# A decoder layer on one core: the first block's mean and variance in one-column instructions, and new sequences for all engines

## The reference

```python
x = _layernorm(x + attn(x))              # linear attention, width 128, with memory M, z
x = _layernorm(x + xattn(ctx, ctx, x))   # long convolution over the features, 32 heads of 8
x = _layernorm(x + ffn(x))               # 4-bit weights, 512 -> 2 x 1408 -> 512, RMS-normed

def _layernorm(x, axis=-1, eps=1e-05):
    m = jnp.mean(x, axis=axis, keepdims=True)
    v = jnp.var(x, axis=axis, keepdims=True)
    return (x - m) / jnp.sqrt(v + eps)
```

## Time and profile before

| | us |
|---|---|
| three runs: median (lowest to highest) | 527.06 (526.91 to 527.37) |
| the profiled execution | 527.41 |
| its span, first to last instruction | 525.7 |
| TensorE busy | 502.1 |
| VectorE, ScalarE, GpSimd busy | 378.5, 399.1, 384.1 |
| mean granted TensorE clock, share of full | 0.995 |

### The profile page before, as it was taken

How to read it: one execution, slowest core, us unless ns; L and a number is a source line. 1 busy time by engine, 2 the same in 40 slices (tenths; PEclk the granted TensorE clock), 3 DMA queues, 4 the chain that set the end, 5 groups by cost and what they waited for, 6 DMA issues and landing times.

```text
span 525.7 us, 11981 instructions
## 1 busy us (share of the span) xinstructions
PE 502.1 (96%) x3612; PEld 370.2 (70%) x3612; DVE 378.5 (72%) x1161; ACT 399.1 (76%) x962; POOL 384.1 (73%) x449
## 2 busy tenths in 40 slices
...
GB/s 222 182 18 82 131 99 111 109 100 46 1 58 135 144 117 66 39 64 97 66 26 85 67 80 20 83 57 80 22 130 8 40 38 43 2 2 40 1 22 40
DMA packets 91876, 36.45 MB, mean 69 GB/s; under 512 B 73851, under 2 KB 83195, under 8 KB 91835
## 3 DMA queue, kind: packets, MB, share of 16 engines
...
## 4 chain that ended last, share of the span: by engine, by line
PE 75%; ACT 8%; POOL 5%; DVE 4%; issue 3%; DMA 2%; SPq 2%; POOLq 0%; ACTq 0%; DVEq 0%
PE p_n L1271 6%; PE p_n L1270 6%; PE p_n L1269 6%; PE p_cv L129 6%; PE p_cv L131 6%; PE p_cv L130 6%; PE p_x L1256 5%; PE p_qk L1256 4%; PE p_x L1258 4%; PE p_qk L1258 4%; PE p_qk L870 4%; PE p_s L1256 4%; PE p_s L1258 3%; PE p_ct L101 2%; PE p_n L926 2%
## 5 line engine op out<-in xcount | busy, mean ns | idle before, releaser
L1109 ACT ACTIVATE p_qk<-p_qk,rescale 128x256 f32<-128x256 f32 x192 | 80.3, 471 | 22.3 <-PE p_qk L1258 20.8
L129 PE MATMUL p_cv<-kv_hi,toe 128*128 128x288 f16 x320 | 91.5, 286 | 2.3 <-issue 1.3
L131 PE MATMUL p_cv<-kv_hi,toe 128*128 128x288 f16 x320 | 91.5, 286 | 0.0
L130 PE MATMUL p_cv<-kv_lo,toe 128*128 128x288 f16 x320 | 91.5, 286 | 0.0
L1077 POOL TENSOR_TENSOR h_lo<-w,h_hi 128x256 f16<-128x256 f32 x88 | 63.6, 738 | 36.6 <-ACT h_hi L1126 36.5
L1109 ACT ACTIVATE p_x<-p_x,rescale 128x256 f32<-128x256 f32 x192 | 80.9, 480 | 0.6 <-PE p_x L1258 0.2
L283 POOL TENSOR_TENSOR shared<-shared 128x1024 f32<-128x1024 f32 x32 | 76.6, 2393 | 4.4 <-DVE shared L243 4.4
L1269 PE MATMUL p_n<-wd_hi,h_hi 128*128 128x512 f16 x176 | 66.7, 379 | 0.0
L1270 PE MATMUL p_n<-wd_lo,h_hi 128*128 128x512 f16 x176 | 66.7, 379 | 0.0
L1271 PE MATMUL p_n<-wd_hi,h_lo 128*128 128x512 f16 x176 | 66.7, 379 | 0.0
L1256 PE MATMUL p_x<-x_hi,wg_hi 128*128 128x256 f16 x256 | 63.0, 273 | 0.3
(11 more groups left out here) (167 smaller groups left out, 1225.6 us busy)
## 6 DMA issues: line engine op xcount, KB each, us to landing
...
cnat<-in_ctx SPq DMA_DIRECT2D x128, 32.0 KB, 2.0
xq<-x_rows SPq DMA_DIRECT2D x128, 32.0 KB, 2.3
...
```

Source lines behind the costliest of these rows:

```text
L129: nc.tensor.matmul(dst, hi, kh, start=(mb == 0), stop=False)
L130: nc.tensor.matmul(dst, hi, kl, start=False, stop=False)
L131: done = nc.tensor.matmul(dst, lo, kh, start=False, stop=(mb == lb))
L1109: done = nc.scalar.activation(sums, sums, ACT.Copy, scale=rescale[:, p - 1, part * GI + i:part * GI + i + 1])
```

## The change

`means` and `variances` issue two instructions of one column each in place of one of two columns; the semaphore is raised by the second, so that what waits is unchanged. All lists but the end of PE_ORDER, POOL_ORDER and LAST_* are laid out anew; each holds the same steps as before. Number and size of DMAs, matrix products and all other instructions are the same. The diff, cut to the two functions and the beginnings of the first block's lists:

```diff
 
         def means(i):
             dve.wait_ge(z_made, 2 * i + 2)
-            nc.vector.tensor_scalar(negmean[:, i, :], total[:, i, :], -1.0 / D, None, ALU.mult).then_inc(mean_made, 1)
+            for e in range(2):
+                done = nc.vector.tensor_scalar(negmean[:, i, e:e + 1], total[:, i, e:e + 1], -1.0 / D, None, ALU.mult)
+            done.then_inc(mean_made, 1)
 
         def variances(i):
             dve.wait_ge(deviated, 2 * i + 2)
-            nc.vector.tensor_scalar(ve[:, i, :], dev[:, i, :], 1.0 / D, LN_EPS, ALU.mult, ALU.add).then_inc(stats, 1)
+            for e in range(2):
+                done = nc.vector.tensor_scalar(ve[:, i, e:e + 1], dev[:, i, e:e + 1], 1.0 / D, LN_EPS, ALU.mult,
+                                               ALU.add)
+            done.then_inc(stats, 1)
 
         def shift_of_norm(i):
             dve.wait_ge(rs_made, i + 1)
...
-    START_SYNC = ("tw0 x4 x3 cx2 cx3 cx0 cx1 st0 x5 st1 toe0 x6 cx6 st2 st3 xq0 xq1 xq2 xq3 xq4 x7 xr1 cx4 "
-                  "cx7 cx5 toe1 xr0 xq5 xq6 cx8 cx9 toe2 xq7 toe3 xq10 st4 cx12 xr2 cx10 cx11 cx14 xr3 toe4 "
-                  "xq8 xq9 xq11 toe5 st7 st5 st6 cx13 cx15").split()
...
+    START_SYNC = ("cx0 cx2 tw0 x3 x4 cx1 cx3 toe1 cx6 st0 toe0 st1 cx7 x5 x6 st2 st3 cx4 x7 cx5 xq2 xq0 xq1 "
+                  "xq3 xq6 xq7 toe2 xr1 xr0 xq4 xq5 cx8 xr3 xr2 toe3 cx10 cx11 st4 toe4 cx9 xq8 cx12 cx13 "
+                  "toe5 xq9 xq10 xq11 st7 cx14 cx15 st6 st5").split()
...
-    START_PE = ("ze0 Xa0 Xb0 iw0 iw1 iw2 iw3 iz0 Q0 V0 Xa1 S0 M0 Xb1 N0 Q1 T0 w0 Oa0 w1 Ob0 Xa2 w2 S1 w3 V1 "
-                "w4 w5 Xb2 M1 N1 Q2 T1 w6 w7 Oa1 Ob1 w8 Xa3 w9 V2 w10 w11 S2 Xb3 M2 N2 Q3 T2 w12 w13 Oa2 Ob2 "
...
+    START_PE = ("ze0 iw0 Xa0 Xb0 iw1 iw2 iz0 iw3 Q0 V0 Xa1 S0 M0 Xb1 N0 Q1 T0 w0 w1 Oa0 Ob0 w2 Xa2 S1 V1 w3 "
+                "M1 Xb2 N1 w4 w5 Q2 T1 w6 w7 Oa1 Ob1 w8 Xa3 w9 V2 S2 w10 w11 Xb3 M2 N2 Q3 T2 w12 Oa2 w13 Ob2 "
+                "Xa4 w14 w15 V3 w16 S3 w17 Xb4 M3 N3 Q4 T3 Oa3 w18 Ob3 w19 Xa5 w20 V4 S4 w21 Xb5 M4 N4 w22 "
...
-    START_DVE = ("ze0 is0 u0 sg0 mk0 ig0 dn0 sk0 o0 u1 ra0 sg1 rb0 mk1 u2 bm0 dn1 o1 bn0 kt0 nb0 ra1 rb1 bm1 "
-                 "sg2 bn1 mk2 kt1 dn2 nb1 o2 fs0 ra2 rb2 sg3 bm2 mk3 dn3 u3 o3 u4 sg4 ra3 rb3 bm3 mk4 kl0 "
-                 "bn2 bn3 dn4 nb2 nb3 o4 wl22 wl23 wl24 wl25 ra4 rb4 wl26 wl27 sg5 wl28 mk5 wl29 wl30 bm4 "
-                 "dn5 kl1 kq0 wl31 bn4 wl32 kq1 tm0 tm1 o5 sg6 tm2 tm3 tm4 tm5 kl2 tm6 tm7 ra5 rb5 bm5 mk6 "
-                 "tm8 tm9 kt2 kt3 kl3 tm10 tm11 tm12 tm13 dn6 tm14 o6 tm15 kl4 bq0 kq2 kq3 sg7 ra6 rb6 +tm0 "
-                 "nb4 +tm1 mk7 nq0 bq1 xl0 nq1 dn7 bm6 o7 xl1 +lk1 bn5 +tm2 ra7 +tm3 +tm4 +tm5 rb7 +gu0 +lk2 "
-                 "+gu1 +tm6 +gu2 +tm7 +tm8 +tm9 +tm10 +lk3 +kt0 +tm11 +gu3 bm7 +tm12 +gu4 +gu5 +tm13 +tm14 "
-                 "+tm15 nb5 +kt1 +gu6 +gu7 +bs0 +bn0 bn6 bn7 +bs1 +bn1 +gu8 +nm0 +nm1 +gu9 +ln +gu10 +xt0 "
...
+    START_DVE = ("ze0 is0 u0 sg0 mk0 ig0 dn0 sk0 o0 u1 sg1 ra0 rb0 bm0 mk1 u2 dn1 bn0 kt0 o1 nb0 ra1 rb1 kt1 "
+                 "sg2 mk2 bm1 fs0 dn2 bn1 o2 nb1 ra2 rb2 sg3 mk3 bm2 dn3 u3 o3 u4 ra3 rb3 bm3 sg4 bn2 bn3 "
+                 "mk4 nb2 nb3 kl0 dn4 o4 wl22 wl23 wl24 wl25 ra4 rb4 bm4 wl26 wl27 sg5 wl28 mk5 wl29 wl30 "
+                 "kq0 dn5 kl1 wl31 wl32 kq1 tm0 tm1 bn4 o5 tm2 tm3 tm4 sg6 tm5 kl2 tm6 tm7 mk6 ra5 rb5 nb4 "
+                 "tm8 tm9 kt2 kt3 kl3 bm5 tm10 tm11 tm12 tm13 dn6 bq0 bn5 tm14 tm15 o6 kl4 kq2 kq3 sg7 ra6 "
+                 "rb6 +tm0 nq0 +tm1 mk7 bq1 xl0 dn7 nq1 bm6 o7 xl1 +lk1 +tm2 +tm3 +tm4 bn6 +tm5 +tm6 +gu0 "
+                 "+lk2 +gu1 +gu2 +tm7 +tm8 ra7 +tm9 +tm10 rb7 +kt0 +tm11 +gu3 +lk3 +gu4 +gu5 bm7 +tm12 +tm13 "
+                 "+kt1 +tm14 +tm15 +gu6 +gu7 nb5 +bs0 +bn0 +bs1 bn7 +bn1 +gu8 +nm0 nb6 +gu9 +nm1 +gu10 +xt0 "
...
-    START_ACT = ("xa0 kw0 kw1 xb0 kw2 kw3 re0 vk0 ge0 xa1 ks0 xb1 lc0 ok0 re1 wh0 wh1 wh2 wh3 xa2 vk1 xb2 "
-                 "qs0 lc1 wh4 wh5 ok1 re2 wh6 wh7 wh8 wh9 qs1 xa3 vk2 wh10 xb3 lc2 nm0 wh11 ok2 re3 wh12 "
-                 "wh13 wh14 hk0 wh15 xa4 vk3 wh16 xb4 nm1 lc3 qs2 ok3 re4 wh17 wh18 wh19 wh20 qs3 vk4 wh21 "
-                 "xa5 xb5 wh22 wh23 lc4 nm2 nm3 ok4 wh24 wh25 re5 wh26 wh27 xa6 wh28 wh29 vk5 hk1 wh30 xb6 "
-                 "qs4 wh31 wh32 re6 lc5 ok5 hk2 hk3 vk6 xa7 lc6 hk4 xb7 qs5 ok6 re7 +tl nm4 vk7 xh0 +hk1 "
-                 "+ho1 lc7 xh1 ok7 +rs0_1 +rs1_1 +rs2_1 +rs0_2 +rs1_2 +rs2_2 +rs0_3 +rs1_3 +hk2 +gu0 +rs2_3 "
...
+    START_ACT = ("xa0 kw0 kw1 xb0 kw2 kw3 re0 ge0 vk0 xa1 xb1 lc0 ok0 ks0 re1 wh0 wh1 qs0 vk1 xa2 wh2 wh3 "
+                 "xb2 wh4 wh5 lc1 ok1 wh6 nm0 wh7 re2 wh8 wh9 xa3 vk2 xb3 qs1 lc2 wh10 ok2 wh11 wh12 re3 "
+                 "wh13 nm1 wh14 wh15 xa4 vk3 xb4 wh16 qs2 lc3 wh17 hk0 ok3 re4 wh18 wh19 wh20 qs3 xa5 vk4 "
+                 "wh21 xb5 nm2 nm3 lc4 wh22 wh23 ok4 wh24 wh25 re5 hk1 wh26 wh27 wh28 vk5 xa6 wh29 wh30 xb6 "
+                 "wh31 wh32 qs4 re6 lc5 ok5 hk2 nm4 hk3 vk6 xa7 qs5 xb7 hk4 lc6 ok6 re7 vk7 +tl xh0 +hk1 lc7 "
+                 "xh1 qs6 ok7 +rs0_1 +rs1_1 +rs2_1 +rs0_2 +rs1_2 +rs2_2 +rs0_3 +rs1_3 +hk2 +gu0 +rs2_3 +hh0 "
+                 "+gu1 +ho0 +gu2 +ho1 +rs3_1 +rs4_1 +rs5_1 +hh1 +rs3_2 +rs4_2 +hk3 +rs3_3 +rs4_3 +rs5_2 +hh2 "
...
-    START_POOL = ("id0 ms0 ws0 ws1 ws2 ws3 ws4 ws5 ws6 ws7 pw0 ws8 ws9 ws10 ws11 ws12 pw1 ws13 pr0 ws14 ws15 "
-                  "ws16 ws17 ws18 ws19 ws20 ws21 ws22 ws23 ws24 pw2 pw3 ws25 pr1 ws26 ws27 ws28 ws29 ws30 "
-                  "ws31 ws32 pw4 pr2 tr0 pr3 tr1 pr4 tr2 tr3 pq0 +pr1 pq1 +pr2 +tr0 +hl0 +pr3 +tr1 +hl1 pw5 "
-                  "+hl2 +hl3 +tr2 +hl4 +hl5 +tr3 +hl6 +pn +bn0 +bn1 +hl7 +hl8 +hl9 +hl10 pw6 pw7 +a0 +b0").split()
+    START_POOL = ("id0 ms0 ws0 ws1 ws2 ws3 ws4 ws5 ws6 pw0 ws7 ws8 ws9 ws10 ws11 pr0 pw1 ws12 ws13 ws14 ws15 "
+                  "ws16 ws17 ws18 ws19 ws20 ws21 ws22 pw2 pw3 ws23 ws24 ws25 pr1 ws26 ws27 ws28 ws29 ws30 "
+                  "ws31 ws32 pr2 pw4 tr0 pr3 tr1 pr4 tr2 pq0 tr3 +pr1 pw5 pq1 +pr2 +tr0 +hl0 +pr3 +tr1 +hl1 "
+                  "+hl2 +hl3 +tr2 +hl4 +hl5 pw6 +tr3 +pn +hl6 +bn0 +bn1 +hl7 +hl8 +hl9 +hl10 pw7 +a0 +b0").split()
...
```

More of the change, by code:

```diff
@@ L1346, in decoder_layer @@
-    PE_ORDER = ("y1_0 y1_1 y1_2 g0_0 g1_0 g2_0 y1_3 g0_1 g1_1 y1_4 y1_5 y1_6 g0_2 g1_2 c2 g2_1 g0_3 g1_3 c3 "
[3 rows of a table removed]
-                "g10_3 xt0 y0_6 y0_7 y0_8 y0_9 xt1 y0_10 d1").split()
-    DVE_ORDER = ("tm0 tm1 lk1 tm2 gu0 gu1 tm3 tm4 tm5 lk2 tm6 tm7 tm8 gu2 gu3 tm9 tm10 gu4 lk3 tm11 tm12 kt0 "
-                 "gu5 tm13 bs0 kt1 tm14 gu6 gu7 a1 tm15 b1 kq0 bn0 ln bs1 gu8 nm0 bn1 gu9 gu10 xt0 nm1 e1 "
-                 "xt1 a0 b0 kq1 e0").split()
-    ACT_ORDER = ("tl rs0_1 rs1_1 rs2_1 rs0_2 rs1_2 hk1 rs0_3 rs1_3 ho0 rs2_2 gu0 gu1 hh0 hh1 rs3_1 rs4_1 hk2 "
-                 "rs3_2 rs4_2 rs2_3 rs3_3 rs4_3 gu2 gu3 hh2 hh3 hk3 gu4 rs5_1 rs6_1 rs5_2 rs7_1 hh4 rs6_2 "
-                 "rs7_2 rs5_3 gu5 hh5 rs6_3 rs7_3 gu6 gu7 n1 rs8_1 rs9_1 rs10_1 kn rs8_2 rs9_2 hh6 rs8_3 "
-                 "rs10_2 ho1 gu8 rs9_3 rs10_3 hh7 hh8 gu9 gu10 xt0 hh9 hh10 xt1 n0").split()
@@ L1358, in decoder_layer @@
-    POOL_ORDER = ("pr1 pr2 hl0 hl1 tr0 pr3 hl2 hl3 tr1 tr2 hl4 hl5 pn a1 tr3 hl6 bn0 hl7 hl8 bn1 hl9 hl10 b1 "
+    START_SYNC = ("cx0 cx2 tw0 x3 x4 cx1 cx3 toe1 cx6 st0 toe0 st1 cx7 x5 x6 st2 st3 cx4 x7 cx5 xq2 xq0 xq1 "
+                  "xq3 xq6 xq7 toe2 xr1 xr0 xq4 xq5 cx8 xr3 xr2 toe3 cx10 cx11 st4 toe4 cx9 xq8 cx12 cx13 "
+                  "toe5 xq9 xq10 xq11 st7 cx14 cx15 st6 st5").split()
+    START_PE = ("ze0 iw0 Xa0 Xb0 iw1 iw2 iz0 iw3 Q0 V0 Xa1 S0 M0 Xb1 N0 Q1 T0 w0 w1 Oa0 Ob0 w2 Xa2 S1 V1 w3 "
[9 rows of a table added]
+                "+xt1 +y0_10 +d0 +d1").split()
@@ new lines, in decoder_layer @@
+    START_DVE = ("ze0 is0 u0 sg0 mk0 ig0 dn0 sk0 o0 u1 sg1 ra0 rb0 bm0 mk1 u2 dn1 bn0 kt0 o1 nb0 ra1 rb1 kt1 "
[7 rows of a table added]
+                 "+ln +a0 nb7 +xt1 +b0 +kq0 +e0 +kq1").split()
+    START_ACT = ("xa0 kw0 kw1 xb0 kw2 kw3 re0 ge0 vk0 xa1 xb1 lc0 ok0 ks0 re1 wh0 wh1 qs0 vk1 xa2 wh2 wh3 "
[8 rows of a table added]
+                 "+hh8 +kn +gu10 +hh9 +xt0 +hh10 nm5 +xt1 +n0 nm6 nm7").split()
+    START_POOL = ("id0 ms0 ws0 ws1 ws2 ws3 ws4 ws5 ws6 pw0 ws7 ws8 ws9 ws10 ws11 pr0 pw1 ws12 ws13 ws14 ws15 "
+                  "ws16 ws17 ws18 ws19 ws20 ws21 ws22 pw2 pw3 ws23 ws24 ws25 pr1 ws26 ws27 ws28 ws29 ws30 "
+                  "ws31 ws32 pr2 pw4 tr0 pr3 tr1 pr4 tr2 pq0 tr3 +pr1 pw5 pq1 +pr2 +tr0 +hl0 +pr3 +tr1 +hl1 "
+                  "+hl2 +hl3 +tr2 +hl4 +hl5 pw6 +tr3 +pn +hl6 +bn0 +bn1 +hl7 +hl8 +hl9 +hl10 pw7 +a0 +b0").split()
@@ new lines, in decoder_layer @@
+    PE_ORDER = ("y1_0 y1_1 y1_2 g0_0 g1_0 g2_0 y1_3 g0_1 g1_1 y1_4 y1_5 g0_2 g1_2 y1_6 g2_1 c2 g0_3 g1_3 c3 "
[3 rows of a table added]
+                "g10_3 xt0 y0_6 y0_7 y0_8 y0_9 xt1 y0_10 d1").split()
+    DVE_ORDER = ("tm0 tm1 lk1 tm2 gu0 gu1 tm3 tm4 tm5 lk2 tm6 tm7 tm8 gu2 gu3 gu4 tm9 lk3 tm10 tm11 kt0 tm12 "
```

(6 more changed lines are left out.)

18 lines of the change are left out of this document (8 added, 10 removed), and 32 rows, old and new, of tables (LAST_PE, PE_ORDER, START_ACT, START_PE).

## The result

The changed kernel takes 521.93 us (median of four, 521.24 to 522.45), the kernel before 527.12 on the same chip (526.91 to 527.37): a ratio of 0.9901, with a 95% interval from 0.9883 to 0.9918. The gain is 5.2 us, where 2.3 were forecast, and 0.3 us more than the range held. The profiled execution took 521.24 us, its span is 519.5 (before 525.7).

What follows compares the result with a forecast made beforehand. TensorE, busy 96% of the span, was taken as the bound, with 13.5 us of holes to gain from. Span 525.7 - 0.4 - 1.5 - 0.4 = 523.4, plus 1.7 less 0.35 gave 524.8 us; range 522.2 to 527.3.

Steps and rivals of the forecast that it cites:

- part 4: 85 to 127 us: VectorE limits, c15 starts unchanged, Xb7's 0.45 us stays; -0.4 us together with Part 2 and Part 3.
- rival C: Before c8: the early toe1 pays in full, its 1.33 us stay won, 523.5 us; chance 0.12.
- Part 1: One-column means and variances: the wait beside GpSimd goes, worth 0 to 1.8 us, 1.3 taken.
- rival D: At bm1: one-column instructions wait too, up to 0.9 us on the path, 524.8 to 525.7 us; chance 0.07.
- Part 2: Up to Q3 in the new order: early steps later, then made good, Q3 at 41.45 to 41.7; term -0.3 us.
- (a): At the start: iz0 ahead of iw3, whose four transposes come behind it, puts Q0 some 0.3 us later.
- Part 3: Up to c0 (85 us), loads of xq: tm0 0.3 us earlier, kq0 holds little, no further gain.
- rival A: Before c0: kq0 blocks VectorE and with it wl32 and c0, 5.1 us, run 530.0 us; chance 0.08.
- Part 5: 127 to 172 us: earlier xr3 and xr2 bring bs1 and xt0 forward; -1.5 us, from 0 to at most 1.9.
- Part 6: The periods: half of rt1's 0.8 us wait in the first full one goes, -0.4 us; 0 in the others.
- Rival B: No change: another wait takes xr3's place and 1.1 us of early delays aren't made good, 527 within 1; chance 0.15.

Runs made afterwards that it cites:

- sum of parts: Kernel before with one-column means and variances, toe1 behind cx1, xr3 and xr2 behind xq7, new lists of periods and end, other first-block lists old: 521.51 us.

## Why the prediction was wrong in its size

**The step that failed is part 4**, "the stretch is VectorE's ..., so c15 starts when it did", with -0.4 us for parts 2 to 4. Measured at +g0_0: -3.2. The busy share of the earlier trace rows was read as a limit that nothing in the change would move. It did move. The 38.7 busy us of 42 held waits: beside the times of the kernel before it says that waits are counted as idle, but that is true of waits for a semaphore only, while an instruction that has begun and waits beside GpSimd counts as busy. With toe1 there in time, VectorE lost its 0.57 us of idle before tm8, kl3 went from 2.27 to 1.60 us in the changed kernel (1.58 with toe1 alone), and c15 came 2.0 us earlier. L732 went from 1.45 to 0.25 us (0.41), T6 follows with no idle, and Oa6 came 3.5 us earlier. The early toe1 alone gives 2.8 us in the old lists by the medians.

That was rival C. Its 1.33 us stayed won at c8, as it said, but not for its reason that the terms are no limit: VectorE was idle for less than half of them, and kl3's shorter wait made up for the rest. The 1.0 us or so of L732 no rival named, and the forecast counted neither wait. The 0.45 us that it kept for Xb7 can't be set apart: slot 7's early steps are worth nothing in the old lists and 4.6 us in the new ones.

The other terms, by their own steps:

- **Part 1** was right for the old lists: 1.3 forecast, Q3 -1.36. In the new lists the form is worth 6.5 us (528.48 against 521.93), since these put bm beside GpSimd more often. One-column instructions took 0.154 us at most in 32; rival D is refuted.
- **Part 2**: (a) +0.3 came as forecast, Q2 +0.6 instead of +1.1, and Q3 41.13 instead of 41.45.
- **Part 3**: c0 -0.6, tm0 -0.8, instead of -0.3. nm3 was done by 67.3, and kq0 waited 0.86 us for xq at 80.45, ahead of dn5, kl1 and wl31; TensorE stood 0.30 us before c0. That is less than rival A needs, but I had written that a VectorE that stands before kq0 would prove me wrong, and it stood. This trace is also the most favourable: in the four other traces of the new lists with one-column means and toe1 early, kq0 waited 1.66 to 2.02 us and TensorE 1.11 to 1.47 before c0. The longest, from the run with xr2 and xr3 late:

```profile
81.57 0.71 DVE L209 STREAM_TRANSPOSE qv<-xq 128x512 f32<-128x512 f32 x1 [2.02 <-DMA xq<-x_rows]
...
85.33 0.30 PE L129 MATMUL p_cv<-kv_hi,toe 128*128 128x288 f16 x1 [1.47 <-DVE wd_lo L771]
```

  In the sum of parts, with kq0 in its old place, neither waits. So the new place of kq0 may well cost the changed kernel about 1 us in most executions; the new lists with kq0 behind kl1, as before, weren't tried.
- **Part 5**: -2.0 us between +g0_0 and +d0, forecast -1.5 and at most 1.9. xr3 went at 118.7, not 123, and the 3 us before bs1 are gone. The load alone gave 1.1 us by starts and 0.6 by the medians; the rest isn't separated.
- **Part 6**: -0.35 at period 3 as forecast; LAST_* brought 0.6 more at the end, where I had 0. The lists of the periods alone show the same 0.6 there. Which of its steps does it is open.
- **Rival B** was wrong: nothing took xr3's place.

Against the forecast, at the end: part 4's -2.8, part 5's -0.5 and the last period's -0.6 are 3.9 us in the trace, and 2.9 in the medians.
